# Two low-rank layers moved to transposed activations in groups of 512 tokens, on one Trainium2 core

## The chip, the core and the metric

The kernel is one program on one core of a Trainium2 chip. The core has TensorE (PE, with its weight loads shown as PEld), VectorE (DVE), ScalarE (ACT), GpSimd (POOL) and SyncE (SP), which here only asks for transfers. The metric is the device time of one execution in microseconds; less is better.

## What is computed

Four layers, each added to the running activations x of 64 sequences of 32 tokens with 512 features, all in fp32. The change concerns the second and third, and the way from them into the fourth.

```python
x = x + _L0(x, weight0, ids0)            # one 512x512 matrix of 8 for each sequence
x = x + _L1(x, W1, bias1, A1, B1, s, ids1)   # x W1^T + bias + s[id] * ((x A1[id]^T) B1[id]^T), rank 16, 8 adapters
x = x + _L2(x, W2, b2, A2, B2, ids2)     # x W2^T + b + 2 * ((x A2[id]) B2[id]), rank 16, 32 adapters
x = x + _L3(x, Wq, Wk, Wv, Wo, ...)      # projections, RMS norm, rotary, paged attention, output projection
```

## The kernel before

The program runs five stages: the first layer (`layer0`), the two low-rank layers (`lora_layers`), the projections with the attention (`qkv_and_attention`), and the output projection. The first three are blocks that all engines leave together: no engine starts the next block until each has ended its part of this one.

Every product is done three times, on a high and a low part of both operands (`three_pass`, lines 99 to 103: high x high, high x low, low x high). ACT makes the high part by a copy to fp32r, DVE the low part by a subtraction. So each new operand passes ACT and then DVE before PE may use it.

`layer0` (line 143) walks 22 tiles of 4 sequences. SP asks for the rows of a tile with 4 requests (line 238), and ACT and POOL store the sums to a scratch `x1` in DRAM (line 218). POOL ends the block when all stores have landed.

`lora_layers` (line 444) walks 16 tiles of 128 tokens, as a software pipeline of two layers. One pass of the loop on PE is: `low_rank(0)` (12 matmuls of 128 columns: 4 pieces of 128 features, three passes), 4 transposes for layer 2, `base(0)` (12 matmuls of 512 columns with the activations as the stationary side), `delta(0)` (3 of 512 columns), `low_rank(1)` (12 of 128 columns with a 64 wide stationary side), 4 transposes of the next input, `base(1)` and `delta(1)`. POOL adds the bias (line 566), DVE adds the product. The adapters of layer 2 are gathered for each tile by 8 requests on SP, one for A and one for B of each of the 4 sequences (lines 528 and 530), into one buffer. `load_adapters` waits with `ab_split` until DVE has split the last tile's adapters. The first `low_rank` waits for three splits of first weights; DVE makes these behind a mask that needs six small loads (lines 655 to 662). At the end SP waits for all stores (line 552), and the block ends.

`qkv` (line 767 on) reads the result back from DRAM, 16 tiles of 128 tokens (line 838), and transposes each on PE (line 1116) between the 12 matmuls of the 16 first tiles. ACT and DVE split it into `xt_hi` and `xt_lo`, which stay for the whole stage. It also loads its first weights only after the block has begun (line 841). Its tiles 0 to 15 are the first half of the values; nothing of the change touches what follows them.

Of the kernel before, what the change touches and what calls it, by code (L numbers as in the profile page):

```python
# [25 lines left out]
P = 128  # L26
# [43 lines left out]
Both = namedtuple("Both", "ident ident_ready step ps_s ps_pt ps_o ps_y ps_t mm_done normed_ready rotated_ready out_ready stored v_stored")  # L70
# [48 lines left out]

NT0 = (NSEQ + NAD0 * (SPT - 1)) // SPT  # L120
# [22 lines left out]
def layer0(nc, y_stored_pool, x_in, ids, const, w, x_out):  # L143
# [8 lines left out]
    with ExitStack() as ctx:  # L152
        m = Mem(nc, ctx, "l0")
        ident = m.sb("ident", [P, P])
# [4 lines left out]
        ids_sb, ids_f, const_sb = m.sb("ids", [NSEQ, 1], i32), m.sb("ids_f", [NSEQ, 1]), m.sb("const", [NSEQ, width])  # L159
        own = m.sb("own", [NSEQ, NAD0])  # L160
        more, quads = m.sb("more", [NSEQ, NAD0, NSEQ // SPT]), m.sb("quads", [NSEQ, NAD0])
        lower, start = m.sb("lower", [NSEQ, NAD0, NAD0]), m.sb("start", [NSEQ, NAD0])
        place, slot, at_slot = m.sb("place", [NSEQ, NAD0]), m.sb("slot", [NSEQ, 1]), m.sb("at_slot", [NSEQ, SLOTS])
        number, empty = m.sb("number", [1, SLOTS]), m.sb("empty", [1, SLOTS])
        src_f, dst_f = m.sb("src_f", [1, SLOTS]), m.sb("dst_f", [1, SLOTS])
        used, nth_f = m.sb("used", [1, NAD0]), m.sb("nth_f", [1, NAD0])
        named, order_f = m.sb("named", [1, NAD0, NAD0]), m.sb("order_f", [1, NAD0])
        started, adapter_f = m.sb("started", [1, NT0, NAD0]), m.sb("adapter_f", [1, NT0])
        src, dst = m.sb("src", [1, SLOTS], i32), m.sb("dst", [1, SLOTS], i32)

        order, adapter = m.sb("order", [1, NAD0], i32), m.sb("adapter", [1, NT0], i32)
        w_stage = m.sb("w_stage", [P, STAGES, KC, D])
        w_hi, w_lo = m.sb("w_hi", [P, NAD0, KC, D], fp32r), m.sb("w_lo", [P, NAD0, KC, D], fp32r)
        x_sb, y_sb = m.sb("x", [P, XB, D]), m.sb("y", [P, XB, D])
        xt_hi, xt_lo = m.sb("xt_hi", [P, 2, KC, P], fp32r), m.sb("xt_lo", [P, 2, KC, P], fp32r)
# [3 lines left out]
        zeroed, ident_ready = m.sem("zeroed"), m.sem("ident_ready")  # L179
# [40 lines left out]
        with nc.Block(no_gpsimd_drain=True) as block:  # L220
            @block.sync
            def _(sp):
# [33 lines left out]
                tiles(sp, load_next)  # L256

# [186 lines left out]
def lora_layers(nc, x_in, i, x_out):  # L444
# [7 lines left out]


    ROWS = (NAD1 * RANK, SPT * RANK)
    with ExitStack() as ctx:
        m = Mem(nc, ctx, "lora")
        ident = m.sb("ident", [P, P])
        w_in, w_hi, w_lo = m.sb("w_in", [P, 2, KC, D]), m.sb("w_hi", [P, 2, KC, D], fp32r), m.sb("w_lo", [P, 2, KC, D], fp32r)
        a1_in, b1_in = m.sb("a1_in", [P, KC, P]), m.sb("b1_in", [P, D])
        a2_in, b2_in = m.sb("a2_in", [P, SPT, KC, RANK]), m.sb("b2_in", [ROWS[1], D])  # L460
        a_hi = [m.sb(f"a{l}_hi", [P, KC, ROWS[l]], fp32r) for l in range(2)]
        a_lo = [m.sb(f"a{l}_lo", [P, KC, ROWS[l]], fp32r) for l in range(2)]
        b_hi = [m.sb(f"b{l}_hi", [ROWS[l], D], fp32r) for l in range(2)]
        b_lo = [m.sb(f"b{l}_lo", [ROWS[l], D], fp32r) for l in range(2)]
        bias_sb, ids_sb, ids_f = m.sb("bias", [P, 2, D]), m.sb("ids", [P, NSEQ], i32), m.sb("ids_f", [P, NSEQ])
        ids2_sb, own_sb = m.sb("ids2", [1, NSEQ], i32), m.sb("own", [ROWS[1], SPT])
        slots_sb, factor_sb = m.sb("slots", [P, 1]), m.sb("factor", [P, 1])
        mask = m.sb("mask", [P, NSEQ])

        x_sb, xb_sb = m.sb("x", [P, 2, D]), m.sb("xb", [P, 2, D])  # L470
        out_sb = m.sb("out", [P, D])
        xt_hi, xt_lo = m.sb("xt_hi", [P, 2, KC, P], fp32r), m.sb("xt_lo", [P, 2, KC, P], fp32r)
        low = [m.sb(f"low{l}", [ROWS[l], P]) for l in range(2)]
        low_hi = [m.sb(f"low{l}_hi", [ROWS[l], P], fp32r) for l in range(2)]
        low_lo = [m.sb(f"low{l}_lo", [ROWS[l], P], fp32r) for l in range(2)]
        ps_t, ps_low, ps_y = m.ps("ps_t", [P, 2, KC, P]), m.ps("ps_low", [P, 2, D]), m.ps("ps_y", [P, 2, D])

        zeroed, ident_ready = m.sem("zeroed"), m.sem("ident_ready")
        small_loaded, ids2_loaded, weights_loaded = m.sem("small_loaded"), m.sem("ids2_loaded"), m.sems("weights_loaded", 4)
        weights_hi, weights_split = m.sem("weights_hi"), m.sem("weights_split")  # L480
        ids_ready, mask_ready = m.sem("ids_ready"), m.sem("mask_ready")
        x_loaded, ab_loaded = m.sem("x_loaded"), m.sem("ab_loaded")
        ab_hi_done, ab_split = m.sem("ab_hi_done"), m.sem("ab_split")

        xt_done = m.sems("xt_done", 2)
        xb_ready = m.sems("xb_ready", 2)
        hi_done, split_done = m.sems("hi_done", 2), m.sems("split_done", 2)
        low_done = m.sems("low_done", 2)
        masked, low_hi_done, low_split = m.sems("masked", 2), m.sems("low_hi_done", 2), m.sems("low_split", 2)
        mm_done, y_ready = m.sems("mm_done", 2), m.sems("y_ready", 2)  # L490
        y_stored = m.sem("y_stored")
        weights = [(w_in[:, 0, :, :], w_hi[:, 0, :, :], w_lo[:, 0, :, :], i["w1"]),
                   (a1_in[:, :, :], a_hi[0][:, :, :], a_lo[0][:, :, :], i["a1"]),
                   (b1_in[:, :], b_hi[0][:, :], b_lo[0][:, :], i["b1"]),
                   (w_in[:, 1, :, :], w_hi[:, 1, :, :], w_lo[:, 1, :, :], i["w2"])]
        smalls = [(bias_sb[:, 0, :], i["bias1"]), (bias_sb[:, 1, :], i["bias2"]), (ids_sb[:, :], i["ids1"]),
                  (slots_sb[:, :], i["slots1"]), (factor_sb[:, :], i["factor1"]), (own_sb[:, :], i["own2"])]

        def iterations(eng, body, before_l2=lambda: None):

            body(0)
            before_l2()
            with eng.Fori(1, NT - 2) as n:
                body(n)
            for n in range(NT - 2, NT + 1):
                body(n)

        def is_tile(t):

            return not isinstance(t, int) or 0 <= t < NT  # L510

        with nc.Block(no_gpsimd_drain=True) as block:
            @block.sync
            def _(sp):
                def load_x(t):
                    if later(t, 1):
                        sp.wait_ge(xt_done[0], t)
                        sp.wait_ge(xb_ready[0], t)
                    sp.dma_start(x_sb[:, 0, :], x_in[bass.ds(t * P, P), :]).then_inc(x_loaded, 16)

                def load_adapters(t):
                    _, adapters = nc.values_load_multi_w_load_instructions(
                        ids2_sb[0:1, bass.ds(t * SPT, SPT)], engines=[mybir.EngineType.SP],
                        min_val=0, max_val=NAD2 - 1, skip_runtime_bounds_check_because="ids are adapters")
                    if later(t, 1):
                        sp.wait_ge(ab_split, t)
                    for s, a in enumerate(adapters):
                        sp.dma_start(a2_in[:, s, :, :].rearrange("p k r -> p (k r)"), i["a2"][bass.ds(a, 1)])\
                          .then_inc(ab_loaded, 16)
                        sp.dma_start(b2_in[s * RANK:(s + 1) * RANK, :], i["b2"][bass.ds(a, 1)]).then_inc(ab_loaded, 16)  # L530

                load_x(0)
                for n, (buf, _, _, src) in enumerate(weights):
                    sp.dma_start(buf, src).then_inc(weights_loaded[n], 16)
                    if n == 0:
                        for small, small_src in smalls:
                            sp.dma_start(small, small_src).then_inc(small_loaded, 16)
                        sp.dma_start(ids2_sb[:, :], i["ids2"]).then_inc(ids2_loaded, 16)
                load_x(1)
                sp.wait_ge(ids2_loaded, 16)  # L540

                def iteration(n):
                    if is_tile(n):
                        load_adapters(n)
                    if is_tile(n + 2):
                        load_x(n + 2)
                    if is_tile(n - 1):
                        sp.wait_ge(y_ready[1], n)
                        sp.dma_start(x_out[bass.ds((n - 1) * P, P), :], out_sb[:, :]).then_inc(y_stored, 16)

                iterations(sp, iteration)
# [215 lines left out]
def qkv(nc, m, place, both, ahead, x_in, w_all, lens, inv_freq, step_pos, norm_w, q_t, k_t, v_own):  # L767
# [68 lines left out]
    def sync(sp):  # L836
# [8 lines left out]
        for t in range(1, XB):  # L845
            load_x(t)
# [1071 lines left out]
```

## Time and profile before

| | us |
|---|---|
| median of 3 runs | 2536.72 (2536.56 to 2539.2) |
| profiled execution | 2536.5 |
| its span, first to last instruction | 2535.0 |
| first layer | 0 to 106.3 |
| low-rank layers | 106.3 to 297.6 |
| projections: first 16 tiles | 297.6 to 358.0 |

The profile is of one execution. Its page gives busy time by engine; a timeline lists instructions with their start and duration in us and, in brackets, how long the engine was idle before and what released it. Matmuls overlap each other: the step between two starts, not the duration, is what one costs. "x4" merges four instructions. SPq is SP's queue of requests. The granted clock of TensorE is 1.00 at 2.4 GHz and 0.50 at 1.2 GHz.

### The profile page before, as it was taken

Reading aid. Unit: us, or ns where it says so; the run is one execution under the profiler, and the core shown is the slowest. Engines: PE = TensorE matmul, PEld = TensorE weight load, DVE = VectorE, ACT = ScalarE, POOL = GpSimd, SP = SyncE. Lnnn points to the kernel's source line nnn. Section 1 sums busy time; section 2 is a strip of 40 time slices with the busy share of each in tenths; the row PEclk is TensorE's granted clock in tenths of the full one; section 3 lists DMA queues with packets and bytes.
Section 4 is the critical chain, followed back from the end, with each engine's and each line's share of the span. In section 5 each row is a group of like instructions: output and inputs, shape, how many; then the busy total and the mean of one; then the engine's idle time right before and its main releaser. Section 6 shows DMA issues by size and latency. Waiting matters only on the chain. (4 is left out here: it accounts for less than half of the span.)

```text
span 2535.0 us, 55787 instructions
## 1 busy us (share of the span) xinstructions
PE 2425.9 (96%) x16326; PEld 2204.1 (87%) x16327; DVE 1797.9 (71%) x3690; ACT 1590.7 (63%) x3313; POOL 640.9 (25%) x932
## 2 busy tenths in 40 slices
PE   6799899999999979999999999999999997699999
PEld 5578688888888869999999999999999997588887
DVE  5354345988999978878888788788887884544443
ACT  3122235777877778888888888888888884311111
POOL 1222121000000034444444444444444442000000
PEclk9899899999999989999999999999999999899999
DMA  6522342333333469888898888888888974756664
GB/s 223 157 71 79 127 142 88 100 108 106 104 96 103 133 217 300 290 294 300 284 296 301 283 303 290 289 305 280 300 299 282 301 266 169 271 202 216 211 213 147
DMA packets 376142, 541.56 MB, mean 214 GB/s; under 512 B 49394, under 2 KB 263090, under 8 KB 372210
## 3 DMA queue, kind: packets, MB, share of 16 engines
q1 hardware_dynamic: 303922, 316.33, 39.0%
q0 software_dynamic: 70016, 221.30, 25.4%
q10 hardware_dynamic: 2112, 2.89, 0.4%
q8 instruction: 34, 0.56, 0.1%
q14 instruction: 58, 0.48, 0.1%
HBM read 442.06 MB, written 98.30 MB: 213 GB/s over the span
## 5 line engine op out<-in xcount | busy, mean ns | idle before, releaser
L1601 PE MATMUL both_ps_o<-att_pt,att_v 128*128 128x128 f32 x4096 | 539.3, 275 | 0.0
L1299 ACT ACTIVATE att_prob<-att_prob,att_shift 128x544 f32<-128x544 f32 x512 | 384.3, 751 | 205.5 <-DVE att_shift L1319 195.8
L1601 PEld LDWEIGHTS both_ps_o<-att_pt,att_v 128*128 128x128 f32 x4096 | 504.0, 191 | 0.0
L1319 DVE CUSTOM_DVE_ANT_0 att_prob<-both_ps_s,att_mask 128x544 f32<-128x544 f32 x512 | 364.8, 713 | 0.0
L101 PE MATMUL both_ps_s<-att_k_hi,att_q_hi 128*128 128x272 f32 x1024 | 339.3, 331 | 4.8 <-DVE att_k_lo L1294 4.8
L1294 DVE TENSOR_TENSOR att_k_lo<-att_k_raw,att_k_hi 128x1024 fp32r<-128x1024 f32 (+1 forms) x320 | 338.6, 1058 | 1.9 <-ACT att_k_hi L1288 1.9
L1578 PE MATMUL both_ps_pt<-both_ident,att_prob 128*128 128x128 f32 x2048 | 309.2, 274 | 6.6 <-ACT att_prob L1299 5.0
L103 PE MATMUL both_ps_s<-att_k_hi,att_q_lo 128*128 128x272 f32 x1024 | 297.9, 291 | 0.0
L1477 ACT ACTIVATE att_pt<-both_ps_pt 128x512 f32<-128x512 f32 x512 | 294.4, 575 | 2.2 <-PE both_ps_s L1586 1.2
L102 PE MATMUL both_ps_s<-att_k_lo,att_q_hi 128*128 128x272 f32 x1024 | 295.3, 288 | 0.0
L1288 ACT ACTIVATE att_k_hi<-att_k_raw 128x1024 fp32r<-128x1024 f32 (+1 forms) x320 | 292.7, 915 | 0.0
L1413 POOL DMA_DIRECT2D att_vo<-v_own x256 | 139.7, 546 | 556.4 <-PE both_ps_o L1604 495.3
L1419 POOL DMA_INDIRECT att_v<-in_v_pages,att_rows_now x256 | 251.6, 983 | 86.1 <-issue 86.1
L1509 DVE TENSOR_REDUCE att_p_own<-att_prob 128x32 f32<-128x32 f32 x512 | 90.9, 177 | 235.2 <-PE both_ps_s L103 222.1
L1578 PEld LDWEIGHTS both_ps_pt<-both_ident,att_prob 128*128 128x128 f32 x2048 | 242.4, 142 | 7.2 <-ACT att_prob L1299 5.2
L1757 ACT ACTIVATE out_o_hi<-out_o 128x2048 fp32r<-128x2048 f32 x32 | 61.4, 1919 | 290.4 <-DVE out_o L1784 282.7
L101 PE MATMUL out_ps_y<-out_w_hi,out_o_hi 128*128 128x512 f32 x512 | 203.0, 397 | 36.8 <-DVE out_w_lo L1777 31.2
L102 PE MATMUL out_ps_y<-out_w_lo,out_o_hi 128*128 128x512 f32 x512 | 201.8, 394 | 0.0
L103 PE MATMUL out_ps_y<-out_w_hi,out_o_lo 128*128 128x512 f32 x512 | 201.6, 394 | 0.0
L101 PEld LDWEIGHTS both_ps_s<-att_k_hi,att_q_hi 128*128 128x128 f32 x1024 | 195.0, 190 | 6.8 <-DVE att_k_lo L1294 5.2
L1604 PE MATMUL both_ps_o<-att_pto,att_vo 128*128 128x128 f32 x1024 | 198.0, 275 | 0.0
L102 PEld LDWEIGHTS both_ps_s<-att_k_lo,att_q_hi 128*128 128x128 f32 x1024 | 196.0, 191 | 0.0
(191 smaller groups left out, 5160.4 us busy)
## 6 DMA issues: line engine op xcount, KB each, us to landing
att_k_raw<-in_k_pages SPq DMA_DIRECT2D x1024, 128.0 KB, 4.7
q_t<-qkv_out_t SPq DMA_DIRECT2D x128, 256.0 KB, 2.3
att_q_raw<-q_t POOLq DMA_DIRECT2D x64, 512.0 KB, 7.3
o_t<-att_o POOLq DMA_DIRECT2D x64, 512.0 KB, 6.8
out_o<-o_t SPq DMA_DIRECT2D x32, 1024.0 KB, 6.1
out_inv<-inv_t SPq DMA_DIRECT2D x32, 1024.0 KB, 6.5
qkv_w_stage<-in_w_qkv SPq DMA_DIRECT2D x12, 1024.0 KB, 5.1
l_w_stage<-in_w SPq DMA_DIRECT2D x8, 1024.0 KB, 7.2
```

The source lines that it names most:

```text
L101: pe.matmul(out, xh, wh, start=start, stop=False)
L102: pe.matmul(out, xh, wl, start=False, stop=False)
L103: return pe.matmul(out, xl, wh, start=False, stop=stop)
L1288: act.activation(hi, raw, ACT.Copy).then_inc(hi_done, 1)
L1294: dve.tensor_tensor(lo, raw, f32(hi), ALU.subtract).then_inc(lo_done, 1)
L1299: act.activation(prob[:, b, :], prob[:, b, :], ACT.Exp, bias=shift[:, b:b + 1], scale=-1.0, accum_out=total[:, j // HK, j % HK:j % HK + 1] ...
L1319: dve.tensor_tensor_reduce(out=prob[:, b, :].rearrange("p (a n) -> p a n", a=2), in0=ps_s[:, j % 2, :, 0:HALF], in1=mask[:, j // HK, :].re ...
L1419: pool.indirect_dma_start(v_sb[p][:, c, :], None, v_pages.rearrange("n k x -> (n k) x"), bass.IndirectOffsetOnAxis(ap=rows_now[:, p, c:c + ...
L1477: act.activation(pt_sb[:, j % OG, :, :], ps_pt[:, j % 2, :, :], ACT.Copy).then_inc(pt_ready, 1)
L1578: mm = pe.transpose(ps_pt[:, j % 2, c, :], prob[:, j % NB_P, c * P:(c + 1) * P], ident[:, :])
L1601: pe.matmul(out, v_sb[p][:, c, h * DH:(h + 1) * DH], pt_sb[:, j % OG, c, :], start=(c == 0), stop=False)
L1604: pe.matmul(out, vo_sb[p][:, g % 2, j % OG, :], pto_sb[:, g % 2, :], start=False, stop=True).then_inc(pv_done, 1)
```

## The change

- **Orientation.** The low-rank block keeps activations transposed (features on partitions, tokens along the row). Weights become the stationary side, 512 tokens (a group) the moving side. There are 4 groups (`LG`) and 8 rounds, one for each layer and group, in the order of `ROUNDS`. A round is `low_rank`, and then for each of 4 chunks `c` of output features: one turn (4 transposes of a tile, in six of the rounds), `base`, `delta`.
- **Adapters.** Layer 2 takes a group as two halves of 8 sequences, with full 128 wide adapters. SP asks for 16 sequences' A and B together, 32 requests for each group, into a buffer that also holds the first layer's A and B. 
- **Inputs and results.** Inputs are turned once, before layer 1. The result of layer 2 stays split in `xt_hi` and `xt_lo` for the projections, and is also turned back and stored to `x3`, which the output projection reads. The projections no longer load or turn anything.
- **Early weights.** The first low-rank weights (A, W, B of layer 1) are asked for by SP at the end of the first layer, the projections' first weights within the low-rank block. The rooms in SBUF are laid out for it.
- **Bias.** It becomes a per-partition scalar in DVE's addition; POOL has no part left in the block. The loops are written out.

The core of the diff:

```diff
+ROUNDS = [(0, 0), (0, 1), (1, 0), (0, 2), (1, 1), (0, 3), (1, 2), (1, 3)]
+INPUTS_TURNED = {0: 1, 2: 2, 4: 3}
+RESULTS_TURNED = {3: 0, 5: 1, 7: 2}
...
                 tiles(sp, load_next)
+                for buf, weights, loaded in early:
+                    sp.dma_start(buf, weights).then_inc(loaded, 16)
...
+                def load_x(t):
+                    if t >= 4:
+                        sp.wait_ge(turned, TURN_OF["x", t - 4 if t < 6 else t - 2] + 1)
+                    sp.dma_start(x_sb[:, x_buf(t), :], x_in[rows(t), :]).then_inc(x_loaded[x_buf(t)], 16)
+                def load_adapters(g):
+                    for h in range(2):
+                        _, adapters = nc.values_load_multi_w_load_instructions(
+                            ids2_sb[0:1, (2 * g + h) * HS:(2 * g + h + 1) * HS], engines=[mybir.EngineType.SP],
...
+                        if g:
+                            sp.wait_ge(ab_split, 4 * g)
+                        elif h:
+                            sp.wait_ge(weights_split, FIRST_OF[W2])
+                        for s, a in enumerate(adapters):
+                            sp.dma_start(a_in[:, h, s * KC * RANK:(s + 1) * KC * RANK], i["a2"][bass.ds(a, 1)])\
+                              .then_inc(ab_loaded[h], 16)
+                            sp.dma_start(b_in[s * RANK:(s + 1) * RANK, h, :], i["b2"][bass.ds(a, 1)])\
+                              .then_inc(ab_loaded[h], 16)
...
+                for t in range(TPG):
+                    load_x(t)
+                for buf, src in smalls:
+                    sp.dma_start(buf[:, :], src).then_inc(small_loaded, 16)
+                sp.dma_start(ids2_sb[:, :], i["ids2"]).then_inc(ids2_loaded, 16)
+                for t in range(TPG, TPG + 2):
+                    load_x(t)
+                sp.dma_start(w_in[:, 1, :, :], i["w2"]).then_inc(weights_loaded[W2], 16)
                 sp.wait_ge(ids2_loaded, 16)
+                load_adapters(0)
+                for t in range(TPG + 2, TPG + 4):
+                    load_x(t)
+                sp.wait_ge(weights_split, FIRST_OF[B1])
+                sp.dma_start(w_in[:, 0, :, :], w_next).then_inc(kept.w_loaded[0], 16)
+                for g in range(1, LG):
+                    if g < LG - 1:
+                        for t in range(TPG * (g + 1), TPG * (g + 1) + 2):
+                            load_x(t)
+                    load_adapters(g)
+                    if g < LG - 1:
+                        for t in range(TPG * (g + 1) + 2, TPG * (g + 2)):
+                            load_x(t)
+                    for t in range(TPG * (g - 1), TPG * g):
+                        store(t)
...
+                def take_input(t):
+                    act.activation(state[g % 3][:, :, in_group(t)], ps_t[:, turn % 2, :, :], ACT.Copy)
+                    act.activation(xt_hi[:, :, rows(t)], ps_t[:, turn % 2, :, :], ACT.Copy).then_inc(x_hi_done, 1)
+                def copy_result(t):
+                    if t >= 2:
+                        act.wait_ge(both.x_stored[t % 2], 16 * (t // 2))
...
+                for n in range(len(ROUNDS)):
+                    g = adapters_after(n)
+                    apply_mask(n)
+                    low_lo_part(n)
+                    turn(n, 0)
+                    if g is not None:
+                        a_lo_part(g)
+                    for c in range(KC):
+                        add(n, c)
+                        y_lo_part(n, c)
+                        if c + 1 < KC:
+                            turn(n, c + 1)
...
+                    if g is not None:
+                        b_lo_part(g)
...
+                for n in range(len(ROUNDS)):
+                    low_rank(n)
+                    for c in range(KC):
+                        turn(n, c)
+                        base(n, c)
+                        delta(n, c)
+                for t in range(NT - TPG, NT):
+                    transpose("z", t)
```

The last two loops are DVE's and PE's; ACT makes the high parts in the order of DVE's. `adapters_after(n)` is the group whose layer 2 is round n + 1, if there is one. `transpose` of an input waits for its load and for the buffer two turns back. `transpose` of a result waits for all four additions of its group's layer 2. `a_lo_part(g)` and its high part on ACT wait for the loads of group g's adapters. `b_lo_part(g)` raises `ab_split` to 4g + 4, which the next group's `load_adapters` waits for.

## Rows read from the trace of the kernel before

**Rows 1.** The page, busy time and share of each engine:

```profile
PE 2425.9 (96%) x16326; PEld 2204.1 (87%) x16327; DVE 1797.9 (71%) x3690; ACT 1590.7 (63%) x3313; POOL 640.9 (25%) x932
```

**Rows 2.** Timeline of PE: where the low-rank block begins and ends:

```profile
109.23 1.09 PE L698 MATMUL lora_ps_t<-lora_ident,lora_x 128*128 128x128 f32 x4 [7.29 <-DMA lora_x<-x]
119.53 0.47 PE L101 MATMUL lora_ps_low<-lora_xt_hi,lora_a_hi 128*128 128x128 f32 x1 [9.21 <-DVE lora_b_lo L662]
...
293.84 0.39 PE L103 MATMUL lora_ps_y<-lora_b_hi,lora_low_lo 64*128 64x512 f32 x1
...
305.45 0.78 PE L101 MATMUL both_ps_s<-qkv_w_hi,qkv_xt_hi 128*128 128x512 f32 x1
```

**Rows 3.** Timeline, one steady pass of the loop, low-rank to low-rank:

```profile
149.69 0.33 PE L101 MATMUL lora_ps_low<-lora_xt_hi,lora_a_hi 128*128 128x128 f32 x1
...
151.46 0.48 PE L101 MATMUL lora_ps_y<-lora_w_hi,lora_xt_hi 128*128 128x512 f32 x1
...
154.35 0.39 PE L101 MATMUL lora_ps_y<-lora_b_hi,lora_low_hi 128*128 128x512 f32 x1
...
160.02 0.33 PE L101 MATMUL lora_ps_low<-lora_xt_hi,lora_a_hi 128*128 128x128 f32 x1
```

**Rows 4.** Timeline of PE: two tiles of the values with transposes, two without:

```profile
313.33 0.60 PE L1116 MATMUL both_ps_o<-both_ident,qkv_x 128*128 128x128 f32 x4
...
316.51 0.60 PE L1116 MATMUL both_ps_o<-both_ident,qkv_x 128*128 128x128 f32 x4
...
355.24 0.39 PE L101 MATMUL both_ps_pt<-qkv_w_hi,qkv_xt_hi 128*128 128x512 f32 x1
...
357.95 0.39 PE L101 MATMUL both_ps_s<-qkv_w_hi,qkv_xt_hi 128*128 128x512 f32 x1
```

**Rows 5.** Timeline of PE in the attention, matmuls of 272 columns:

```profile
1201.03 0.29 PE L102 MATMUL both_ps_s<-att_k_lo,att_q_hi 128*128 128x272 f32 x1
1201.16 0.29 PE L103 MATMUL both_ps_s<-att_k_hi,att_q_lo 128*128 128x272 f32 x1
```

**Rows 6.** By stretch: busy time of PE, PEld, DVE, ACT, POOL, granted clock, DMA:

```profile
123.00:125.00 2.00, 2.00 (x6) 1.52 (x6) 0.29 (x1) 0.10 (x1) 0.00 (x0) 0.50 0.00 0
125.00:127.00 2.00, 2.00 (x10) 1.59 (x9) 0.00 (x0) 0.00 (x0) 0.00 (x0) 0.98 0.00 0
...
295.00:298.00 3.00, 0.00 (x0) 0.00 (x0) 0.00 (x0) 0.00 (x0) 0.29 (x2) 0.62 0.23 87
```

**Rows 7.** Timeline of PE, matmuls of 512 columns at the low clock:

```profile
290.01 0.63 PE L101 MATMUL lora_ps_y<-lora_w_hi,lora_xt_hi 128*128 128x512 f32 x1
290.44 0.63 PE L102 MATMUL lora_ps_y<-lora_w_lo,lora_xt_hi 128*128 128x512 f32 x1
```

**Rows 8.** Timeline of SP's queue: requests for inputs and adapters:

```profile
106.28 0.37 SPq L519 DMA_DIRECT2D lora_x<-x  x1
...
115.50 0.33 SPq L519 DMA_DIRECT2D lora_x<-x  x1
116.55 0.35 SPq L528 DMA_DIRECT2D lora_a_in<-in_a  x1
116.99 0.38 SPq L530 DMA_DIRECT2D lora_b_in<-in_b  x1
117.55 0.33 SPq L528 DMA_DIRECT2D lora_a_in<-in_a  x1
```

**Rows 9.** DMA view of the low-rank block: count, KB each, median us to landing:

```profile
lora_x<-x SPq DMA_DIRECT2D x16, 256.0 KB, 2.6
x<-lora_out SPq DMA_DIRECT2D x16, 256.0 KB, 2.1
...
lora_a_in<-in_a SPq DMA_DIRECT2D x64, 32.0 KB, 1.7
```

**Rows 10.** View of one tile: ns least/median/most, first and last start:

```profile
L584 ACT ACTIVATE lora_xt_hi<-lora_ps_t x32: 572/577/597, 113.8 to 284.6; 128x512 fp32r<-128x512 f32 x32
L619 DVE TENSOR_TENSOR lora_xt_lo<-lora_ps_t,lora_xt_hi x32: 673/675/690, 117.6 to 286.6; 128x512 fp32r<-128x512 f32 x32
```

More of the change, by code:

```diff
@@ L466, in lora_layers @@
[L466 to L474, printed above, removed]
@@ L499, in iterations @@
[L499 to L510, printed above, removed]
+        w_hi, w_lo = low_part.sb("w_hi", [P, 2, KC, D], fp32r), low_part.sb("w_lo", [P, 2, KC, D], fp32r)
+        state = [low_part.sb(f"state{n}", [P, KC, GT]) for n in range(2)] + [kept.w_stage[:, 1, :, :]]
@@ new lines, in x_buf, with x_loads, tokens, rows @@
+        def x_buf(t):
+            return t if t < 4 else t % 2
+        def x_loads(t):
+            return 1 if t < 4 else (t - 4) // 2 + 2
+        def tokens(g):
+            return slice(g * GT, (g + 1) * GT)
+        def rows(t):
+            return slice(t * P, (t + 1) * P)
+        def in_group(t):
+            return slice(t % TPG * P, (t % TPG + 1) * P)
+        def halves(g):
+            return [slice(h * HT, (h + 1) * HT) for h in range(2)]
+        def turn_in(n, at):
+            if n in INPUTS_TURNED:
+                return "x", TPG * INPUTS_TURNED[n] + at
+            if n in RESULTS_TURNED:
+                return "z", TPG * RESULTS_TURNED[n] + at
+            return None, None
@@ L515, in load_x @@
                 def load_x(t):
[L516 to L530, printed above, removed]
@@ L542, in iteration @@
[L542 to L551, printed above, removed]
-                sp.wait_ge(y_stored, 16 * NT)
-            @block.gpsimd
@@ new lines, in b_hi_part, with turn @@
+                def b_hi_part(g):
+                    if g:
+                        act.wait_ge(mm_done, KC * (ROUND_OF[1, g - 1] + 1))
+                    for h in range(2):
+                        act.activation(b2_hi[:, h, :], b_in[:, h, :], ACT.Copy).then_inc(ab_hi_done, 1)
+                def turn(n, at):
+                    kind, t = turn_in(n, at)
+                    if kind == "x":
+                        take_input(t)
+                    elif kind == "z":
+                        copy_result(t)
@@ new lines, in b_lo_part, with turn @@
+                def b_lo_part(g):
+                    for h in range(2):
+                        dve.wait_ge(ab_hi_done, 4 * g + 2 + h + 1)
+                        dve.tensor_tensor(b2_lo[:, h, :], b_in[:, h, :], f32(b2_hi[:, h, :]), ALU.subtract)\
+                           .then_inc(ab_split, 1)
+                def turn(n, at):
+                    kind, t = turn_in(n, at)
+                    if kind == "x":
+                        x_lo(t)
+                split_weights_lo(A1)
+                for t in range(TPG):
+                    x_lo(t)
@@ new lines, in low_rank @@
+                def low_rank(n):
+                    l, g = ROUNDS[n]
+                    if n >= 2:
+                        pe.wait_ge(masked, n - 1)
+                    out = ps_low[:, n % 2, :]
+                    if l:
+                        pe.wait_ge(y_split, KC * (ROUND_OF[0, g] + 1))
+                        for h, at in enumerate(halves(g)):
+                            pe.wait_ge(ab_split, 4 * g + h + 1)
+                            for k in range(KC):
+                                last = three_pass(pe, out[:, at], a2_hi[:, h, k, :], a2_lo[:, h, k, :],
+                                                  y_hi[:, g % 2, k, at], y_lo[:, g % 2, k, at], k == 0, k == KC - 1)
+                    else:
+                        pe.wait_ge(x_split, TPG * (g + 1))
+                        if n == 0:
+                            pe.wait_ge(weights_split, FIRST_OF[A1] + 1)
+                        for k in range(KC):
+                            last = three_pass(pe, out, a1_hi[:, k, :], a1_lo[:, k, :],
+                                              xt_hi[:, k, tokens(g)], xt_lo[:, k, tokens(g)], k == 0, k == KC - 1)
+                    last.then_inc(low_done, 1)
@@ L751 @@
+                for t in range(NT - TPG, NT):
+                    transpose("z", t)
 W3 = 2 * (HQ + 2 * HK) * DH // (2 * D)
```

563 lines of the change are left out of this document (276 added, 287 removed).

## The prediction, made before the changed kernel was run

> **What bounds the kernel now.** I read the page's busy shares first: PE is busy for 96% of the span and DVE for 71% [rows 1]. So time moves with PE's own work or with its gaps. Then I looked at where PE stands in the part that changes. The low-rank block begins at 106.28, when SP asks for the first input [rows 8]. PE gets its first transposes at 109.23 and its first `low_rank` at 119.53, released by DVE's last split of weights. Its last matmul starts at 293.84, and the first of the projections at 305.45 [rows 2]. Between those ends the loop is dense: one pass takes 160.02 - 149.69 = 10.33 us without a pause [rows 3]. So the block is bound by PE's steps, with three weak places: its start, its end, and the low clock after each. The granted clock is 0.50 at 123 to 125 and back at 125 (0.98): about 5.5 us after the start at 119.53 [rows 2, 6]. It also falls within the gap after 293.84, where the mean of 295 to 298 is 0.62 with no matmul.
>
> **Prices on PE.** A matmul costs its step between starts. A tile of 12 matmuls with 512 columns takes 357.95 - 355.24 = 2.71 us, 0.226 each; with four transposes before it 3.18, so a turn costs 0.47 [rows 4]. In the low-rank loop 12 such take 2.89 with a slow first one, nearer 0.234 each [rows 3]. I take 0.23. At the low clock a step is 0.43 [rows 7], so 5.5 us at that level do the work of 2.9; I book 2.6 for each fall of the clock. For 256 columns the nearest row is the attention's 272, step 0.13 [rows 5]; scaled by columns that is 0.12.
>
> **The new rounds.** One chunk is 15 matmuls: 3.41 us, with a turn 3.88. A layer 1 round is 12 x 0.23 + 4 x 3.41 = 16.4 without turns and 18.3 with them. In layer 2 the low-rank part is 24 x 0.12 = 2.8 and the delta 6 x 0.12, which is the same. Six rounds have turns: 6 x 18.3 + 2 x 16.4 = 142.6 us, against 16 x 10.33 = 165.3 now. The small matmuls of 128 columns, which cost half a step of 512 for a quarter of the columns, are what goes.
>
> **The start.** The early weights are asked for behind the last inputs of layer 0, so they hide under its last tiles. Their loads leave room; if they slowed that layer's stores, the 1.5 MB would cost some 4 us, for which no row speaks, so I book nothing. The mask no longer stands before them. What is late next is the first group: four inputs instead of one, each needing two copies on ACT and one subtraction on DVE (0.58, 0.58, 0.68 [rows 10]). Two turn buffers pace it: pair one is split at about 113.4, pair two at 116.4. So `low_rank(0)` starts at 116.4 instead of 119.53. At the low clock it takes 12 x 0.43 = 5.1, to 121.5; two chunks later it is 129.3.
>
> **SP's queue is the step that decides.** An adapter pair (A and B) is asked for every 1.00 us (116.55 to 117.55 [rows 8]), although a load lands 1.7 after its request [rows 9]. Now 4 pairs stand against a pass of 10.3 us. After the change 16 pairs stand in one train, and the input tiles 2 and 3 of the next group stand behind it. Reading the eight registers of a half costs something more: 116.55 is 0.7 after the end of the request before it, for four. I take 0.9 between the halves, with bounds 0 and 1.4.
> - Round 0. SP needs until about 112.6 for four inputs, six small loads, two inputs and W2 (0.42 to 0.55 each), the ids land by 114, and the train ends at 114 + 0.9 + 8 + 0.9 + 8 = 131.7. Tile 6 lands 2.6 later [rows 9], at 134.3. PE wants it at 129.3: stall 5.0, and the clock falls, 2.6. Round 0 ends at 129.3 + 5.0 + 7.8 + 2.6 = 144.7, round 1 at 161.1.
> - Round 2 wants tile 10 at 2.8 + 7.8 = 10.6 after its begin. `load_adapters(1)` may start only when `b_lo_part(0)` has run. That is 3.6 after round 1's end: addition 0.9, high part 0.7, two B high parts and the last B low part 2.0. Then 8 + 0.9 + 8, and the landing of tile 10, 2.6: 23.0. Stall 12.4, and 2.6 for the clock. Tiles 12 and 13 for round 4 make it by about 1 us.
> - Round 4 is the same with tile 14: 15.0.
> - Round 7. The last train starts 3.6 after round 5, and its second half lands at 3.6 + 8 + 0.9 + 8 + 1.7 = 22.2. But `a_hi_part(3)` and `a_lo_part(3)` stand before round 6's four additions on ACT and DVE. They end at 23.6, and the additions follow with 2.05 for each chunk (0.69 + 0.58 + 0.68 and the steps between), the last at 30.5. PE has done round 6 at 16.4 and, after 2.8 of `low_rank`, would turn result tile 8 at 19.2. That turn waits for all four additions: stall 11.3, clock 2.6, together 13.9.
>
> Sum of the stalls: 7.6 + 15.0 + 15.0 + 13.9 = 51.5 us. The rounds end at 116.4 + 2.4 (the cold first `low_rank`) + 142.6 + 51.5, about 313 (313.2 by steps). That is 19 later than 294.1, where they end now.
>
> **The end and the projections.** Four result tiles are still turned, copied and stored. The copies of tiles 14 and 15 wait until the stores of 12 and 13 have landed (2.1 [rows 9]), and the block ends 6.6 after the last round. The projections' first weights are already there, so only one high and one low part stand before the first matmul: 1.5. It starts at 321.3, 8.1 after the last round, against 11.3 now. Sixteen tiles then take 16 x 2.71 + 2.7 for the low clock = 46.1; now it is 357.95 - 305.45 = 52.5. Later tiles were never turned. DVE's angles and the values' second weights come well before tile 16.
>
> Sum: +19.1 - 3.2 - 6.4 = +9.5 us. The profiled execution took 2536.5, 0.2 under the median; the forecast is 2546.
>
> A rule against this count stands in the Trainium skill, "DMA: Bandwidth & Descriptors", section "Anatomy of one DMA - SWDGE (gpsimd) path": the sequencer needs some 50 ns to dispatch a transfer. It is told there of GpSimd's path. By it a train of 32 would be an estimated 1.6 us. This trace does not agree for SP: 0.33 to 0.38 busy, 0.50 from one to the next [rows 8].
>
> **Rivals.**
> - A, the other side: the train costs far less than its rows say. It decides at a request step of 0.42: each 0.01 takes 32 x 4 x 0.01 = 1.3 us from the sum, so 9.5 are gone at 0.42, and at about 0.32 rounds 0 and 7 no longer wait. At 0.1 no stall is left: 2546 - 51.5 = 2494.5. Against it: every adapter row repeats the 1.00 [rows 8]. For it: none of these trains is longer than four pairs, and it is what the skill's dispatch time would give. Chance 0.13.
> - B: the stalls are there, but the clock costs nothing or little in them. 4 x 2.6 less: 2536. Against it: the clock fell within two to three us of a silent PE after 293.84 [rows 6]. Chance 0.12.
> - C: some of the four waits are shorter because I lag in a chain (the release of `ab_split`, or round 7's additions). Without round 7's, 2532; without it and half of another, about 2525. Chance 0.10.
> - D: the chains of ACT and DVE at each chunk's end, with margins of 0.3 to 1 us, do not fit. Some 1 us in each of 8 rounds and longer landings: 2556 to 2565. Chance 0.08.
> - The forecast, with its four stalls: 0.57, own range 2536 to 2556. The bounds: 480 matmuls of 512 columns at 0.226 or 0.234 are -2 or +2; the register reads -4 or +2; landings of 1.7 to 3.0 for the three tiles -3 to +1; falls of the clock at 2.0 to 2.9 each -2 to +1.
>
> **How the numbers follow.** The range takes B, C and D in and leaves most of A out: 2518 to 2562. A measurement of this kernel can tell about 0.2%, 5 us. Slower by more: three quarters of the forecast's 0.57 and D, 0.50. Within: the rest of it, most of B and part of C, 0.22. Faster: A, and what is left of B and C, 0.28.
>
> **What would show it.** In the changed kernel's timeline: `low_rank(0)` at about 116; gaps of PE before transposes of `lora_x`, about 5 us at 129 and 12 us near 172 and 224, each released by a DMA, with clock 0.50 after it. A gap of some 6 us in `low_rank` near 282, released by DVE `a2_lo`, and one more before z's turn. SP's queue should show trains of 32 at 0.50. The first projection matmul stands near 321, and its tiles step by 2.71 without L1116. If the gaps are absent, SP's pace (A) is wrong; if the gaps stand but matmuls after them step by 0.23, the clock (B) is.

## The result, and the profile after

The changed kernel takes 2545.43 us (median of 7 runs, 2543.68 to 2548.3), the kernel before beside it 2537.9 (2536.56 to 2539.2): ratio 1.003, 95% interval 1.0019 to 1.0041. It is slower by 7.5 us; the forecast was 2546. The profiled execution of after took 2544.21 us with a span of 2542.6, 7.7 more than the profiled one of before (2536.5).

The page of after, to be read beside [rows 1]. PE is busy for 16.9 us less, and the span is 7.6 longer. The change does take work off PE, and puts idle time in its place.

```profile
span 2542.6 us, 54643 instructions
PE 2409.0 (95%) x16070; PEld 2195.2 (86%) x16071; DVE 1780.3 (70%) x3632; ACT 1602.2 (63%) x3311; POOL 599.9 (24%) x896
```

PE's waits in the low-rank block of after (engine, tile and line that waited, what it waited for: us in total, times, longest). The first row holds the start of the block (7.4) and the waits for inputs 6, 10 and 14.

```profile
PE lora_ps_t L798 <- DMA lora_x<-x: 36.8, 4, 12.2
PE lora_ps_low L102 <- DVE lora_a_lo L741: 4.8, 1, 4.8
PE both_ps_s L102 <- DVE qkv_w_lo L1123: 4.5, 1, 4.5
PE lora_ps_t L798 <- DVE both_w_stage L728: 4.1, 1, 4.1
```

The timeline of PE in after, where it stood idle. The number in brackets is the idle time before the row, with its releaser. The rows answer to [rows 2].

```profile
109.25 1.94 PE L798 MATMUL lora_ps_t<-both_ident,lora_x 128*128 128x128 f32 x8 [7.38 <-DMA lora_x<-x]
...
116.24 0.79 PE L102 MATMUL lora_ps_low<-both_xt_hi,lora_a_hi 128*128 128x512 f32 x1 [1.90 <-DVE both_xt_lo L703]
...
133.91 1.08 PE L798 MATMUL lora_ps_t<-both_ident,lora_x 128*128 128x128 f32 x4 [5.46 <-DMA lora_x<-x]
...
184.28 1.09 PE L798 MATMUL lora_ps_t<-both_ident,lora_x 128*128 128x128 f32 x4 [12.20 <-DMA lora_x<-x]
...
234.78 1.09 PE L798 MATMUL lora_ps_t<-both_ident,lora_x 128*128 128x128 f32 x4 [11.75 <-DMA lora_x<-x]
...
286.19 0.46 PE L102 MATMUL lora_ps_low<-lora_y_hi,lora_a_hi 128*128 128x256 f32 x1 [4.80 <-DVE lora_a_lo L741]
...
293.10 1.08 PE L798 MATMUL lora_ps_t<-both_ident,both_w_stage 128*128 128x128 f32 x4 [4.09 <-DVE both_w_stage L728]
...
311.63 1.06 PE L798 MATMUL lora_ps_t<-both_ident,lora_state 128*128 128x128 f32 x8 [0.94 <-DVE lora_state L728]
...
318.56 0.80 PE L102 MATMUL both_ps_s<-qkv_w_hi,both_xt_hi 128*128 128x512 f32 x1 [4.46 <-DVE qkv_w_lo L1123]
...
364.70 0.39 PE L102 MATMUL both_ps_s<-qkv_w_hi,both_xt_hi 128*128 128x512 f32 x1
```

Five waits of the rounds stand there, 38.3 us together (5.46 + 12.20 + 11.75 + 4.80 + 4.09). The last row is the first matmul of tile 16, which stood at 357.95 before [rows 4]: 6.75 later, which is nearly the whole difference.

SP's queue in after, the train for the second group's adapters and the inputs behind it, 10 and 11 (as [rows 8]):

```profile
164.87 0.34 SPq L576 DMA_DIRECT2D lora_a_in<-in_a  x1
165.31 0.38 SPq L578 DMA_DIRECT2D lora_b_in<-in_b  x1
165.87 0.33 SPq L576 DMA_DIRECT2D lora_a_in<-in_a  x1
...
172.23 0.38 SPq L578 DMA_DIRECT2D lora_b_in<-in_b  x1
173.34 0.33 SPq L576 DMA_DIRECT2D lora_a_in<-in_a  x1
...
181.44 0.88 SPq L564 DMA_DIRECT2D lora_x<-x  x2
```

A pair is asked for every 1.00 us, the two halves stand 1.11 apart, and the inputs are asked for 16.6 us after the train's first request. PE, which waits for the first of them, goes on at 184.28, 2.84 us after the request.

The clock in after (columns: stretch, its length, then busy time of PE, PEld, DVE, ACT and POOL, the granted clock, the DMA share, GB/s). First the start, then behind the waits for inputs 6 and 10, where it is 0.50 and 0.58, then 1.00:

```profile
118.00:120.00 2.00, 2.00 (x8) 1.53 (x8) 1.61 (x4) 0.05 (x1) 0.00 (x0) 0.73 0.67 178
134.00:138.00 4.00, 4.00 (x12) 3.32 (x13) 0.69 (x1) 1.08 (x2) 0.00 (x0) 0.50 0.85 284
184.00:188.00 4.00, 3.72 (x12) 3.18 (x13) 0.69 (x1) 1.08 (x2) 0.00 (x0) 0.58 0.06 21
188.00:192.00 4.00, 4.00 (x24) 3.42 (x23) 1.42 (x2) 1.33 (x3) 0.00 (x0) 1.00 0.00 0
```

### The profile page after: what moved, and what is told of

Its sections match the earlier page's. It is cut to its first block and busy times, and to the rows that moved or that the text cites. A ratio compares the mean times of both kernels' runs of the same rounds, so it can differ in the third digit from the quotient of the medians.

```text
span 2542.6 us, 54643 instructions
## 1 busy us (share of the span) xinstructions
PE 2409.0 (95%) x16070; PEld 2195.2 (86%) x16071; DVE 1780.3 (70%) x3632; ACT 1602.2 (63%) x3311; POOL 599.9 (24%) x896
## 3 DMA queue, kind: packets, MB, share of 16 engines
q1 hardware_dynamic: 301538, 311.62, 38.2%
```

## The experiments

The theory: SP's train of 32 requests, at 0.50 each, makes the five waits of PE, and each long wait costs something more at the low clock. Rival A says that the requests are not what takes the time, rival B that the clock costs nothing. Then there are single steps: round 7's additions, the early weights.

The first four kernels ran on a chip where the kernel before takes 2628.2 us (2626.0 to 2634.16), the others on one where it takes 2538.1. Differences are taken against kernels on the same chip. Waits and positions up to the first projection matmul are compared across both.

**e1: one request in the place of sixteen.** It always takes adapters 0 to 7, so the choice of the adapters is left out; bytes, buffers and waits stay.

```diff
-for s, a in enumerate(adapters):
-    sp.dma_start(a_in[:, h, s * KC * RANK:(s + 1) * KC * RANK], i["a2"][bass.ds(a, 1)])...
-    sp.dma_start(b_in[s * RANK:(s + 1) * RANK, h, :], i["b2"][bass.ds(a, 1)])...
+sp.dma_start(a_in[:, h, :].rearrange("p (s k) -> p s k", s=HS), i["a2"][0:HS].rearrange("s p k -> p s k"))...
+sp.dma_start(b_in[:, h, :], i["b2"][0:HS].rearrange("s r d -> (s r) d"))...
```

> The changed kernel with one request of 256 KB for A and one for B of each half of a group, from fixed adapters 0 to 7, in place of 8 and 8: the same bytes into the same rooms, 4 requests for a group where there were 32. It leaves out the choice of adapters, so layer 2 gets wrong ones. Forecast's theory (the count of requests on SP's queue makes the four stalls): the gaps before tiles 6, 10 and 14 and the wait in round 7 all go, with the low clock behind them; 2545 - 51 = 2494 us, and at most 2500. Rival (it is the bytes, or the release by ab_split that comes only at a round's end, that is late): the gaps stay, at least 8 of 12 us at tiles 10 and 14, and the time is over 2530.

Measured: 2588.32 us, 39.9 under before, ratio 0.9853 (0.9836 to 0.9869). The theory's 2494 to 2500 was 38 to 44 under before, so it holds. SP's queue shows what is left of the train in e1, the same bytes asked for in 2.1 us:

```profile
158.38 0.38 SPq L575 DMA_DIRECT2D lora_a_in<-in_a  x1
158.80 0.58 SPq L577 DMA_DIRECT2D lora_b_in<-in_b  x1
159.43 0.43 SPq L575 DMA_DIRECT2D lora_a_in<-in_a  x1
159.90 0.58 SPq L577 DMA_DIRECT2D lora_b_in<-in_b  x1
160.52 2.07 SPq L564 DMA_DIRECT2D lora_x<-x  x2
```

No wait of PE is left in the rounds, and the first projection matmul stands 156.05 us after `low_rank(0)` (272.68 - 116.63), 202.3 in after (318.56 - 116.24). So the number of requests makes all five waits, and with what they bring they cost 46 us. The e1 requests also have fixed addresses, but one of them takes SP no less than before: 0.42 from A to B (158.80 - 158.38), 0.44 in after (165.31 - 164.87). These trains too begin only when `ab_split` is raised, so the late release, the other half of the rival, makes no wait either.

**e2: the inputs ahead of the train.** SP asks for all four inputs of the next group first, then for the adapters. At the start, which the cut of the diff does not show, inputs 6 and 7 stand between the two halves of group 0's adapters.

```diff
-for t in range(TPG * (g + 1), TPG * (g + 1) + 2):
+for t in range(TPG * (g + 1), TPG * (g + 2)):
     load_x(t)
 load_adapters(g)
-if g < LG - 1:
-    for t in range(TPG * (g + 1) + 2, TPG * (g + 2)):
-        load_x(t)
```

> The changed kernel with the same requests in another order: tiles 6 and 7 between the two halves of group 0's adapters, tiles 10, 11 and 14, 15 ahead of groups 1's and 2's adapters. Forecast's theory: the gaps of 5.5, 12.2 and 11.8 us go with about 2.6 us of low clock behind each, round 7's wait stays: 2545 - 37 = 2508 us. Rival (later groups' adapters then come too late for ScalarE and VectorE, so the wait only moves): over 2525 us, with PE waiting in low_rank of rounds 4 and 6.

Measured: 2601.09 us, 27.1 under before, ratio 0.9896 (0.988 to 0.9913). 30 were expected. The three waits for inputs are gone, and only round 7's two remain, about as long as in after. The timeline of PE in e2:

```profile
253.25 0.58 PE L102 MATMUL lora_ps_low<-lora_y_hi,lora_a_hi 128*128 128x256 f32 x1 [4.75 <-DVE lora_a_lo L739]
260.15 1.09 PE L796 MATMUL lora_ps_t<-both_ident,both_w_stage 128*128 128x128 f32 x4 [3.98 <-DVE both_w_stage L726]
```

So for the inputs only their place behind the train matters; for round 7 it is the train itself. What round 7 costs can be read here: e2 needs 168.2 us from `low_rank(0)` to the first projection matmul (285.55 - 117.34), e1 156.05. That is 12.2 for two waits of 8.7 and the low clock.

**e3: as e2, with the B rows asked for by GpSimd, and the A parts behind a round's second chunk.** The cut shows DVE's A part; ScalarE's moves likewise.

```diff
+@block.gpsimd
+def _(pool):
+    ...
+            for s, a in enumerate(adapters):
+                pool.dma_start(b_in[s * RANK:(s + 1) * RANK, h, :], i["b2"][bass.ds(a, 1)]).then_inc(b_loaded[h], 16)
...
-    if g is not None:
-        a_lo_part(g)
     for c in range(KC):
...
+        if g is not None and c == 1:
+            a_lo_part(g)
```

> As the reordered kernel, and B's requests go out from GpSimd, which is idle in this block, with a semaphore of their own; and the splits of A stand after the second chunk of a round, not before the first. Forecast's theory: the last train is halved, the additions of round 6 are no longer behind it, and all four stalls are gone: 2494 to 2499 us. Rival (GpSimd's requests, 0.54 us each, or their landing are too slow and round 7 or the deltas wait): 2505 us or more.

Measured: 2587.59 us, 40.6 under before, ratio 0.9843 (0.9826 to 0.9859). PE has no wait in the rounds. It ran once more on the second chip, beside the changed kernel:

> e3 once more, as the companion of e5 and of the changed kernel. Same as its first run: ratio 0.983 to 0.986 against before, no gap of PE of 1 us or more in the rounds, and 45 to 50 us below the changed kernel if the five waits and the low clock behind them are all that the requests cost.

Measured: 2497.93 us (2496.55 to 2499.23), ratio 0.9846 (0.983 to 0.9863), 50.3 under the changed kernel there. It leaves out no part of the computation, and it beats both kernels: 40 us under before. GpSimd's half of a train in it, twice eight requests, each eight in 4.5 us:

```profile
158.54 4.52 POOL L621 DMA_DIRECT2D lora_b_in<-in_b  x8 [33.92 <-DVE lora_b_lo L762]
163.77 4.51 POOL L621 DMA_DIRECT2D lora_b_in<-in_b  x8 [0.71 <-issue]
```

From one request to the next GpSimd takes 0.58 us (158.54 to 159.12 in this trace), so it asks no faster than SP. What e3 gains are three steps together: with the order of the inputs alone the kernel is 27.1 under before (e2), and the two others bring the remaining 13.5. Each of these two alone leaves a wait in round 7, as e7 and e8 show.

**e4: the changed kernel with 50 matmuls of 512 columns, which nobody reads, before the turns of inputs 10 and 14.** PE stays at work while it waits, so that only the clock changes.

```diff
+if kind == "x" and t in (10, 14):
+    for _ in range(50):
+        pe.matmul(ps_t[...], w_hi[:, 0, 0, 0:P], xt_hi[:, 0, tokens(t // TPG - 1)], start=True, stop=True)
```

> The changed kernel with 50 matmuls of 512 columns (50 x 0.23 = 11.5 us) put on PE in each of the two long gaps, before the turns of tiles 10 and 14; their sums go to a turn buffer that the transposes overwrite, so nothing of the result changes. The gaps are as long as before, but PE is busy in them. If the low clock behind a stall costs 2.6 us each as the forecast booked: 2545.4 - 5.2 = 2540 us. Rival B (the clock costs nothing in the stalls): 2545 us. If the filler is longer than the gap it would be over 2545.

Measured: 2630.28 us, ratio to before 1.0007 (0.9997 to 1.0017). The changed kernel's ratio is 1.003, and 0.0023 of 2628 is 6.0 us. But these are two chips. The traces say less: from `low_rank(0)` to the first projection matmul e4 takes 199.2 us (317.92 - 118.73), and the changed kernel 201.8 to 203.4 in its three runs, so the two falls of the clock that the filler takes away cost 2.6 to 4.2 together. The next two runs gave the changed kernel on the second chip.

**e6 and e10: the changed kernel on the second chip**, as the companion of the others.

> The changed kernel itself, so that it stands on the same chip as its variants. On the first chip it was 7.5 us slower than before (ratio 1.003). Both theories (request step with clock, request step alone) expect the same here: +4 to +10 us against before, with gaps of PE of about 5, 12, 12, 5 and 4 us before the first transposes of inputs 6, 10, 14, the last low_rank and the last result turn, and the first projection matmul about 202 us after low_rank(0). If it is instead within 2 us of e4 (the filler), then the low clock behind the long gaps cost nothing and rival B's step was right; my theory wants it 4 to 6 us above e4's +2.1.

> The changed kernel once more, as the companion of the two others on their chip: 7 to 10 us above before, gaps of 5, 12, 12, 5 and 4 us.

Measured: 2548.19 us (ratio 1.0045, 1.0028 to 1.0062) and 2546.93 (ratio 1.0034, 1.0022 to 1.0047), 10.1 and 8.8 over before. That is 8.0 and 6.7 above e4's 2.1, where 4 to 6 was expected of e6, again more than the traces show. The waits are those of after, but for input 6: 4.59 and 3.06 instead of 5.46. Its train does not hang on a round's end but on the start. From `low_rank(0)` to this wait PE took 12.2, 12.9 and 13.7 us in after, e6 and e10 (128.45 - 116.24, 128.23 - 115.31, 131.40 - 117.69), and the wait is shorter where that is longer.

**e9: the same filler in all five gaps** (20, 50, 50, 20 and 15 matmuls).

> The changed kernel with matmuls of 512 columns that nobody reads in all five gaps (20 before input 6, 50 each before inputs 10 and 14, 20 before the last low_rank, 15 before the first result turn behind it), each train a little shorter than its gap. Theory (behind each long gap 2.6 us go to the low clock): 8 to 11 us under the changed kernel on the same chip, so within 2 us of before, with steps of 0.23 right behind every gap. Rival B (the low clock costs nothing or little): within 2 us of the changed kernel.

Measured: 2541.31 us (2538.07 to 2542.99), ratio 1.0012 (1.0003 to 1.0022), 5.6 under e10. Not all of it is the filler's: from `low_rank(0)` to the first projection matmul e9 takes 198.7 us (313.93 - 115.24), 3.1 to 4.7 less than the three runs of the changed kernel, and `low_rank(0)` itself stands 2.5 earlier than in e10. The same views as of after show the full clock behind each gap:

```profile
134.00:138.00 4.00, 4.00 (x22) 3.29 (x21) 0.99 (x2) 1.08 (x2) 0.00 (x0) 1.00 0.76 268
183.00:187.00 4.00, 4.00 (x24) 3.46 (x23) 1.52 (x3) 0.76 (x3) 0.00 (x0) 1.00 0.00 0
235.00:239.00 4.00, 4.00 (x23) 3.37 (x22) 2.19 (x4) 1.60 (x3) 0.00 (x0) 1.00 0.00 0
287.00:293.00 6.00, 3.62 (x17) 2.73 (x18) 4.38 (x7) 2.79 (x5) 0.00 (x0) 1.00 0.00 0
```

Neither side had it right: not the 8 to 11 of the theory, nor the 2 at most of rival B. PE's work from one gap to the next says why. Input 6's turn to the next gap took 38.2, 37.2 and 36.9 us in after, e6 and e10, and 35.4 in e9; input 10's turn to the next gap 38.8, 40.0 and 39.6, against 37.2. A fall costs 1.5 to 2.8 us there, about 2 in the mean, where 2.6 was booked. And part of what is won is lost again in the waits: in e9 the last A split stands 20.0 us after its train's first request (280.68 - 260.64), 18.8 in after, and input 6 came 18.3 after `low_rank(0)`, 16.8 to 17.7 in the three others. Whether the filler itself or chance delays these two is not settled.

**e7: the A parts behind the second chunk, nothing else.**

> The changed kernel with one move: the a_hi and a_lo parts of the next adapters stand behind the second chunk of a round on ScalarE and VectorE instead of before the first. Theory (round 6's four additions queue behind the A part that waits for the last train, and the last result turn waits for them): the gap before round 7's low_rank stays at about 4.8 us, the 4.1 us before the first result turn behind it goes to 0.5 or less, the other gaps stay, and the time falls by 3.5 to 4.5 us against the changed kernel on the same chip. Rival (the additions are late for another reason, such as the subtraction of the low part or the state's copies): both gaps stay and the time is the same within 1 us.

Measured: 2540.4 us (2535.58 to 2543.39), 7.8 under e6 beside it by the medians, with 10 and 4 runs that scatter by 8 and 4 us; the two profiled executions differ by 5.1 (2540.03 and 2545.17). Expected were 3.5 to 4.5. The stretch from `low_rank(0)` to the first projection matmul agrees with that: 198.9 us (315.62 - 116.74), 2.9 to 4.5 under the three runs of the changed kernel. What more the medians show is not explained. Its timeline of PE where round 7's two waits stood:

```profile
287.65 0.58 PE L102 MATMUL lora_ps_low<-lora_y_hi,lora_a_hi 128*128 128x256 f32 x1 [4.67 <-DVE lora_a_lo L741]
294.95 0.38 PE L102 MATMUL lora_ps_y<-lora_low_hi,lora_b_hi 128*128 128x256 f32 x1 [0.34 <-DVE lora_low_lo L721]
```

The wait for the result's turn is gone, the one for the A part stays at 4.7. So the additions were late only because they stood behind the A part in DVE's and ACT's order. DVE in after shows that queue: the A part ends its wait at 285.45, and the four additions (L728) follow 2.05 apart.

```profile
285.45 0.69 DVE L741 TENSOR_TENSOR lora_a_lo<-lora_a_in,lora_a_hi 128x512 fp32r<-128x512 f32 x1 [8.01 <-ACT lora_a_hi L654]
286.06 0.74 DVE L728 SCALAR_TENSOR_TENSOR both_w_stage<-lora_ps_y,lora_bias,both_w_stage 128x512 f32<-128x512 f32 x1
...
288.11 0.74 DVE L728 SCALAR_TENSOR_TENSOR both_w_stage<-lora_ps_y,lora_bias,both_w_stage 128x512 f32<-128x512 f32 x1
...
292.20 0.74 DVE L728 SCALAR_TENSOR_TENSOR both_w_stage<-lora_ps_y,lora_bias,both_w_stage 128x512 f32<-128x512 f32 x1
```

**e8: the changed kernel with the B rows asked for by GpSimd, nothing else moved.** The train is half as long, as if a request cost 0.25.

> The changed kernel with the requests of the B rows issued by GpSimd, nothing else moved: SP's train is 16 requests instead of 32, so 8 us shorter. Theory (each wait is the train's length beyond PE's work, and falls us for us with it): no gap before input 6 (5.5 - 8 is below nothing), gaps of 4.2 and 3.8 us before inputs 10 and 14 (12.2 - 8, 11.8 - 8), no gap before the last low_rank, about 1 us before the first result turn behind it. The gaps fall by 29.4 us, and one or two falls of the clock (2.6 each) go too: 32 to 37 us under the changed kernel on the same chip, so 24 to 28 under before. Rival (the landing of the data, not its asking, is what takes the time): the gaps stay within 2 us of the changed kernel's.

Measured: 2517.84 us (2516.71 to 2519.8), ratio 0.9924 (0.9907 to 0.994), 29.1 under e10. SP's train and PE's waits in e8:

```profile
159.39 8.69 SPq L576 DMA_DIRECT2D lora_a_in<-in_a  x16
168.14 0.90 SPq L564 DMA_DIRECT2D lora_x<-x  x2
```

```profile
171.37 1.08 PE L813 MATMUL lora_ps_t<-both_ident,lora_x 128*128 128x128 f32 x4 [4.76 <-DMA lora_x<-x]
...
214.42 0.63 PE L813 MATMUL lora_ps_t<-both_ident,lora_x 128*128 128x128 f32 x4 [4.43 <-DMA lora_x<-x]
...
264.92 0.63 PE L813 MATMUL lora_ps_t<-both_ident,both_w_stage 128*128 128x128 f32 x4 [2.60 <-DVE both_w_stage L743]
```

The train is 7.8 us shorter (8.75 instead of 16.57 to the inputs' request), and the waits for inputs 10 and 14 are 7.4 and 7.6 shorter than in e10. So they follow it us for us, and the rival, that landing takes the time, falls. The result turn kept 2.6 where 1 was expected, and 1.1 more stand behind it (waits for `lora_low_lo`). PE does not wait in that round's `low_rank` any more and reaches the turn sooner, while the four additions still need their 2.05 each. Also, e10 had less to give than after, whose waits the expectation took: its wait for input 6 was 3.06 and not 5.46. So it won 29 and not 32 to 37.

**e5: e3 without the early request for the first weights.** SP asks for them behind the first four inputs of the block.

> As e3, with the three early weight requests given up: they are issued behind the first four inputs of the low-rank block, as before the change. Theory (the early request is worth what ScalarE's first split then waits for): that split waits for a landing near 111.9 and the input copies behind it start some 2 us later, so low_rank(0) starts 2 to 3 us later and the time is 2 to 3 us above e3 on the same chip. Rival 1 (early requests hide nothing, since the inputs pace the start): within 1 us of e3. Rival 2 (the early loads cost layer 0's last stores about 4 us): up to 1 us below e3 or more, with layer 0's last matmul earlier.

Measured: 2499.88 us (2497.49 to 2502.21), 1.95 over e3 beside it; their runs overlap. The traces are plainer. ScalarE's first instructions, in e3 and then in e5:

```profile
106.02 0.63 ACT L629 ACTIVATE lora_a_hi<-lora_a_in 128x512 fp32r<-128x512 f32 x1 [9.41 <-PEq L231]
110.31 0.60 ACT L638 ACTIVATE lora_state<-lora_ps_t 128x512 f32<-128x512 f32 x1 [3.67 <-PE lora_ps_t L811]
```

```profile
111.31 0.63 ACT L631 ACTIVATE lora_a_hi<-lora_a_in 128x512 fp32r<-128x512 f32 x1 [15.79 <-DMA lora_a_in<-in_a]
111.85 0.58 ACT L640 ACTIVATE lora_state<-lora_ps_t 128x512 f32<-128x512 f32 x1
```

In e5 the first split waits for its load, and the first copy of an input, 1.1 us after the first transposes in e3 (110.31 - 109.19), comes 3.8 after them (111.85 - 108.02). `low_rank(0)` follows its first transposes by 9.67 us (117.69 - 108.02) and by 6.98 in e3 (116.17 - 109.19). The early request is worth 2.7 us there, of which the time shows about 2. It is small beside the trains.

## Why the prediction was right, step by step

The time is 0.6 us from the forecast, but that is partly luck. What was forecast is a difference, +9.5, and it came out as +7.5 by the medians and +7.7 by the profiled executions; the kernel before ran at 2537.9 beside the changed one, 1.2 above the median of its first three runs. The mechanism was right: four stalls, three from input tiles behind SP's train and one in round 7, ate what the wider matmuls gave. The terms:

| step | predicted | after |
|---|---|---|
| `low_rank(0)` | 116.4 | 116.24 |
| wait before input 6 | 5.0 | 5.46 |
| wait before input 10 | 12.4 | 12.20 |
| wait before input 14 | 12.4 | 11.75 |
| waits of round 7 | 11.3 | 4.80 + 4.09 |
| low clock behind four waits | 10.4 | about 8 |
| rounds without stalls, start included | 145.0 | 148.2 (e3) |
| end of the rounds | 313.2 | 310.69 |
| from there to the first projection | 8.1 | 7.87 |
| 16 tiles of the values | 46.1 | 46.14 |

The row on the clock is a difference: 310.69 - 116.24 = 194.45 for after's rounds, less 148.2 (e3 from `low_rank(0)` at 116.17 to 264.37) and 38.3 of waits, is 8.0.

- **SP's queue** was right but for the register reads: 1.00 a pair, the train's begin 3.71 us after round 2's (164.87 - 161.16; 3.6 was taken), the turn of its input 23.12 after that begin (184.28 - 161.16; 23.0 was taken). Between the halves 1.11 us pass instead of 0.56 (165.87 - 165.31), so reading eight registers adds 0.55, where 0.9 was taken. Rival A is excluded by these rows. Its end was well seen: e1, where only the number of requests is taken away, is 0.9853 of before, which of 2538.1 makes 2500.8; A said 2494.5. The slope that the prediction gave, 1.3 us for each 0.01 of a request's cost, would make 32 for e8's half train, if all waits lasted; it was 29, since two of them end before.
- **Round 7** was sized 2.4 too high in waiting, although its end came as forecast, 30.2 after round 6's begin (293.10 - 262.91; 30.5 was taken). Round 6 took 16.9 (279.80 - 262.91) where the sum has 16.4. And `low_rank`'s second half ran at the low clock, 2.8 instead of 1.4 us, between the two waits, where it costs nothing. So a fall of the clock inside a chain that waits anyway was free here, which the prediction did not see.
- **The clock** was the mis-sized term: 2.6 for each fall, worked out from one return after 5.5 us [rows 2, 6]. Measured, 1.5 to 2.8 each, in the sum 8 and not 10.4. Of the 8, 1.4 is the free half of round 7's `low_rank`, so some 6.6 are what the low clock really cost. At the start it came back at about 119, 3 us after `low_rank(0)`, and not after 5.1; but in e6 and e10, the same kernel, it came back 4.5 and 6.1 us after (at 119.8 and 123.8, from the mean clock of 0.81 in 119 to 121 of e6 and in 123 to 125 of e10), so 5.1 was within what this kernel does. Rival B, which had all of it at nothing, is wrong as well: e9's block is 3.1 to 4.7 us shorter. The term decides how much slower the change is, not whether: e9 is still 3.2 us over before (interval 1.0003 to 1.0022), where the changed kernel beside it is 8.8 over.
- **The rounds themselves** were 3.2 too short. A chunk with a turn takes 3.94 us in e3 and not 3.88 (two turns of results, 256.33 and 260.27), one without 3.51 and not 3.41 (143.83 to 147.34): a step is 0.234 and not 0.23, the upper end of the prediction's own bounds. Over 24 and 8 chunks that is 2.2; the rest is spread. The sum was thus 3.2 too low here and 4.8 too high in round 7's waits and the clock, and the errors mostly cancel. That the sum came within 2 us owes something to this.
- **The start, the end and the values** came as priced. The prediction booked nothing for what the early loads do to layer 0. The first transposes stand at 109.25 in after and at 109.23 in before [rows 2]. From run to run they stand between 108.0 and 111.8, so a cost of a microsecond would not be seen.

After's train takes 16.6 us (164.87 to 181.44), and in e3 GpSimd needs 0.58 for a request. The rule of the Trainium skill, "DMA: Bandwidth & Descriptors", section "Anatomy of one DMA - SWDGE (gpsimd) path", has some 50 ns for the sequencer's dispatch on GpSimd's path. The runs don't show that part by itself; as the price of a whole request it would be about a tenth of what is paid, on either engine.

- **Rivals C and D** did not come about: none of the four stalls was missing, and PE has no wait over 0.25 us in e3's rounds, so the chains of ACT and DVE at a chunk's end do fit.

## What to carry to other kernels

Loads that are gathered by one small request each cost time on the queue that asks (32 requests were 16.6 us here), and whatever is asked for behind them lands that much later. When work is regrouped into larger pieces the number of requests stays and the longest train grows, so look at what stands behind it: here input tiles on SP, and on DVE four additions that needed none of its data. Asking first for what is needed first, splitting the train over two engines, and putting the wait for late data behind work that is already due turned some 9 us over the kernel before into 40 under it.

## What the runs showed of the hardware

- **Another chip is 3.6% slower, in the attention.** The kernel before takes 2628.2 us on one chip and 2538.1 on the other. The same kernel, e3, first on the slow chip and then on the other, by stretch:

```profile
100.00:400.00 300.00, 283.66 (x1378) 236.02 (x1377) 141.82 (x220) 118.30 (x236) 59.17 (x79) 0.97 0.32 102
1100.00:1500.00 400.00, 379.42 (x3238) 372.14 (x3237) 301.52 (x715) 309.27 (x596) 167.94 (x255) 1.00 0.82 272
```

```profile
100.00:400.00 300.00, 283.87 (x1380) 236.30 (x1379) 143.40 (x223) 120.45 (x242) 58.76 (x78) 0.97 0.31 100
1100.00:1500.00 400.00, 400.00 (x3474) 399.54 (x3473) 325.47 (x770) 333.11 (x640) 180.30 (x275) 1.00 0.88 294
```

  The low-rank block is the same on both. In the attention PE has gaps on the slow chip at the full clock, and 272 GB/s are moved instead of 294. What it is stays open. The ratios agree all the same: e3's is 0.9843 and 0.9846.
- **GpSimd asks at about SP's pace**, 0.58 us against 0.50, and asking at the same time they hardly slow each other: SP's 16 requests take 8.7 us in e8, about half of after's train.
- **The clock's return is not a fixed time.** Behind waits of 3 to 12 us PE lost 1.5 to 2.8 us in the same kernel, and after `low_rank(0)` the level came back 2.9, 4.5 and 6.1 us later in three runs of the changed kernel (after, e6, e10).
